# One core, attention and a quantised layer: the transfers of one queue in another order, and the second batch of y transposed by DRAM and VectorE

## What is computed

```python
Q = einsum('btx,dx->btd', layernorm(x), Wq) + bq
K = einsum('bpx,dx->bpd', ctx, Wk) + bk
attn = softmax(einsum('btd,bpd->btp', Q, K) / sqrt(1024))
x1 = x + einsum('btp,bpd->btd', attn, ctx)
w = nibbles of qweight (4 bits); wbin = 1 where w > 0 else -1
weights = scales[g_idx] * (wbin - zeros[g_idx])        # 1024 x 1024
out = x1 + layernorm(x1) @ weights + bias
```

## Time and profile before

| what | value |
|---|---|
| median of 3 runs | 542.48 us (542.15 to 542.54) |
| the profiled execution | 542.7 us, its span 540.9 us, 1.8 us around it |
| PE busy | 534.5 us, 99% of the span |
| DVE, ACT, POOL busy | 371.2, 280.8, 187.2 us (69%, 52%, 35%) |
| granted TensorE clock | 1.00 in the whole span (2.4 GHz) |
| DMA: whole span | 113.38 MB, 210 GB/s |

### The profile page before, as it was taken

The page is one execution under the profiler, slowest core; times in us unless marked ns, Lnnn a source line. Parts: engine busy times, 40 slices in busy tenths (PEclk is TensorE's granted clock), DMA queues, the critical chain, the costliest instruction groups (busy, mean ns, idle before and its releaser), DMA issues.

```text
span 540.9 us, 7404 instructions
## 1 busy us (share of the span) xinstructions
PE 534.5 (99%) x2638; PEld 447.3 (83%) x2638; DVE 371.2 (69%) x604; ACT 280.8 (52%) x496; POOL 187.2 (35%) x151
## 2 busy tenths in 40 slices
PE   8999999999999999999999999999999999999997
PEld 7788788787777877778898899999888888888886
DVE  4988458886888675782446455574968779778742
ACT  5987955314676681343348566686553244325210
POOL 1064000010000000000327777777865744753530
PEclk9999999999999999999999999999999999999999
DMA  8941893459588646936499999898356775774212
GB/s 262 321 163 41 154 158 78 159 147 319 199 237 281 205 173 195 272 83 189 135 213 304 362 321 353 322 417 315 138 150 240 228 225 189 214 233 136 97 79 78
DMA packets 83156, 113.38 MB, mean 210 GB/s; under 512 B 37072, under 2 KB 59672, under 8 KB 80944
## 3 DMA queue, kind: packets, MB, share of 16 engines
q1 hardware_dynamic: 76592, 106.62, 60.7%
q10 hardware_dynamic: 6528, 6.29, 5.8%
HBM read 70.89 MB, written 41.94 MB: 209 GB/s over the span
## 4 chain that ended last, share of the span: by engine, by line
PE 91%; ACT 4%; DMA 2%; DVE 1%; POOL 1%; issue 1%; ACTq 0%; POOLq 0%
PE bank L1395 25%; PE bank L1397 24%; PE bank L1396 24%; PE bank L1433 4%; PE bank L1439 4%; PE bank L1436 4%; PE bank L1485 2%; DMA cin<-in_ctx 2%; POOL cn_lo L613 1%; PE bank L1411 1%; ACT xjunk_early L735 1%; ACT wq_bk L690 1%; ACT xjunk_early L730 1%; PE bank L1544 1%; PE bank L1514 1%
## 5 line engine op out<-in xcount | busy, mean ns | idle before, releaser
L1395 PE MATMUL bank<-xT_hi,m_hi 128*128 128x512 f32 x256 | 101.0, 395 | 0.0
L1397 PE MATMUL bank<-xT_hi,m_lo 128*128 128x512 f32 x256 | 99.7, 390 | 0.0
L1396 PE MATMUL bank<-xT_lo,m_hi 128*128 128x512 f32 x256 | 99.6, 389 | 0.0
L620 POOL TENSOR_TENSOR tT_lo<-t_pair,tT_hi 128x1024 fp32r<-128x1024 f32 x16 | 38.1, 2399 | 75.2 <-ACT tT_hi L662 75.2
L1347 DVE TENSOR_TENSOR xres<-xres,bank 128x512 f32<-128x512 f32 x56 | 38.3, 683 | 36.1 <-PE bank L1397 36.0
L876 ACT ACTIVATE t_pair<-bank,ucol 128x512 f32<-128x512 f32 x32 | 22.0, 687 | 77.7 <-PE bank L1397 73.1
L634 POOL TENSOR_TENSOR l_lo_s<-l_sum_s,l_hi_s 128x512 fp32r<-128x512 f32 x32 | 40.4, 1295 | 54.9 <-DVE l_sum_s L1275 54.9
L1395 PEld LDWEIGHTS bank<-xT_hi,m_hi 128*128 128x128 f32 x256 | 48.0, 188 | 11.8 <-issue 2.1
L1397 PEld LDWEIGHTS bank<-xT_hi,m_lo 128*128 128x128 f32 x256 | 48.0, 188 | 10.2
L1396 PEld LDWEIGHTS bank<-xT_lo,m_hi 128*128 128x128 f32 x256 | 48.1, 188 | 10.0 <-issue 0.2
L1433 PE MATMUL bank<-wk_hi,wq_hi 128*128 128x512 f32 x128 | 50.4, 394 | 0.2
(11 more groups left out here) (158 smaller groups left out, 1246.6 us busy)
## 6 DMA issues: line engine op xcount, KB each, us to landing
xres<-in_x SPq DMA_DIRECT2D x8, 1024.0 KB, 12.4
out<-xres SPq DMA_DIRECT2D x15, 512.0 KB, 5.0
right_scratch<-part_hi SPq DMA_DIRECT2D x28, 256.0 KB, 2.2
xn_scratch<-xin SPq DMA_DIRECT2D x6, 1024.0 KB, 4.7
xq<-xn_scratch ACTq DMA_DIRECT2D x24, 256.0 KB, 5.4
cin<-in_ctx SPq DMA_DIRECT2D x6, 1024.0 KB, 7.2
r_tile<-right_scratch SPq DMA_DIRECT2D x6, 1024.0 KB, 11.1
yn_scratch<-yin SPq DMA_DIRECT2D x6, 1024.0 KB, 4.0
```

The costliest lines, as they stand in the source:

```text
L620: pool.tensor_tensor(tT_lo[b][:, ks, :], t_pair[b // 2][:, b % 2, ks, :], tT_hi[b % 2 if b else 2][:, ks, :].bitcast(F32), ALU.subtract).t ...
L1395: pe.matmul(out_, a_hi, b_hi, start=start, stop=False, skip_group_check=True)
L1396: pe.matmul(out_, a_hi, b_lo, start=False, stop=False, skip_group_check=True)
L1397: return pe.matmul(out_, a_lo, b_hi, start=False, stop=stop, skip_group_check=True)
```

## The change

There are two parts. In the first, SP's transfers stand in another order: the raw x of batch 5 in stage 2 goes behind the store of the normalised batch 4; in stage 3 the first chunk of right factors goes behind the load of ctx of batch 3 instead of ahead of it, the chunks of slices 0 and 1 are one batch later and smaller at the start (three factors at b = 0 in place of five, and two chunks at b = 5), and the bias rows are loaded at b = 6 instead of b = 1. In the second, y of f = 1 is no longer transposed by TensorE but as those of f of 2 and more: stored, read back, and transposed by DVE. For that its statistics move from behind `invert_sum(B - 1)` into batch 6 of attention, POOL's `rsqrt(B + 1)` ahead of `add_bias(0, ..)`, and ACT's `y_apply(1, ..)` ahead of the high parts of s3 and s4 of f = 0. The reloads go out once the last `pv` is done, since `yq` lies where the high part of ctx lay.

```diff
@@ who has made a block of y @@
-            if f < 2:
-                eng.wait_ge(s_ytr, 4 * f + i + 1)
+            if f < 1:
+                eng.wait_ge(s_ytr, i + 1)
             else:
-                eng.wait_ge(s_yb, 4 * (f - 2) + i + 1)
+                eng.wait_ge(s_yb, 4 * (f - 1) + i + 1)
-        RAW = {2: (4, 5), 6: (6,), 12: (7,)}
+        RAW = {2: (4,), 6: (5, 6), 12: (7,)}
@@ SP, attention @@
-            chunks = {0: ((0, 3, 5),), 1: ((0, 5, 7),), 2: ((1, 0, 3),), 3: ((1, 3, 5),), 4: ((1, 5, 7),),
-                      5: ((2, 0, 3),), 6: ((2, 3, 5), (2, 5, 7))}
+            chunks = {0: ((0, 0, 3),), 1: ((0, 3, 5),), 2: ((0, 5, 7),), 3: ((1, 0, 3),), 4: ((1, 3, 5),),
+                      5: ((1, 5, 7), (2, 0, 3)), 6: ((2, 3, 5), (2, 5, 7))}
                 load_x(b)
-                if b == 0:
-                    load_right(0, 0, 3)
                 if b + 3 < B:
                     load_ctx(b + 3)
...
-                if b == 1:
+                if b == 6:
                     sp.dma_start(bias_rows, ...)
@@ SP, quantised layer @@
+            def rows_of_y_by_quadrant(g):
+                sp.wait_ge(s_yn, QT * (g + 1))
+                sp.dma_start(yn_dram[g]..., yin_of(g)).then_inc(s_ynst, 16)
+                sp.wait_ge(s_ynst, 16 * g)
+                if g == 1:
+                    sp.wait_ge(s_pv, 4 * B)
+                else:
+                    sp.wait_ge(s_yb, 4 * (g - 1))
+                for a in range(4):
+                    sp.dma_start(yq[32 * a:32 * a + 32, :, :], ...).then_inc(s_yql[g % 2], 16)
+            rows_of_y_by_quadrant(1)
             for f in range(B):
...
+                if f + 2 < B:
+                    rows_of_y_by_quadrant(f + 2)
@@ POOL @@
                 ctx_lo(b)
+            rsqrt(B + 1)
...
             ctx_lo(B - 1)
-            rsqrt(B + 1)
@@ ACT @@
                 ctx_hi(b)
+            y_apply(1, 1)
+            y_apply(1, 0)
             act.wait_ge(s_cnlo, 4 * B)
             left_hi(0, "s3")
             left_hi(0, "s4")
-            y_apply(1, 1)
-            y_apply(1, 0)
@@ DVE @@
+                if b == B - 2:
+                    dve.wait_ge(s_x1, 4 * (KH + 2))
+                    y_stats(1)
             p_lo(B - 1)
             invert_sum(B - 1)
-            y_stats(1)
...
                 added(f, 3)
+                if f == 0:
+                    y_blocks(1, "a21")
+                    y_blocks(1, "a22")
+                    added(f, 4)
+                    y_blocks(1, "a11")
+                    y_blocks(1, "a12")
                 if f + 1 < B:
                     left_sum(f + 1, "s1")
                     left_sum(f + 1, "s2")
                     left_lo(f + 1, "a11")
-                added(f, 4)
+                if f > 0:
+                    added(f, 4)
@@ PE @@
                     product(b, n)
                     if b == 0 and n == 1:
                         pv(B - 1)
-                    if b == 0 and n == 3:
-                        y_tr(1, ("a21", "a22", "a11", "a12"))
```

More of the change, by code:

```diff
@@ L535, in _ @@
                 load_last_right(n)
-            for f in range(B):
[L539 to L551, removed]
+            def rows_of_y_by_quadrant(g):
+                sp.wait_ge(s_yn, QT * (g + 1))
+                sp.dma_start(yn_dram[g].rearrange("(t p) f -> p t f", p=P), yin_of(g)).then_inc(s_ynst, 16)
+                sp.wait_ge(s_ynst, 16 * g)
[3 more added lines that the diff above has]
+                    sp.wait_ge(s_yb, 4 * (g - 1))
+                rows = yn_dram[g].rearrange("(m j) f -> j m f", j=32)
+                for a in range(4):
+                    sp.dma_start(yq[32 * a:32 * a + 32, :, :], rows[:, :, a * S:(a + 1) * S]
+                                 ).then_inc(s_yql[g % 2], 16)
+            rows_of_y_by_quadrant(1)
+            for f in range(B):
+                if f + 2 < B:
+                    rows_of_y_by_quadrant(f + 2)
                 for t, n in enumerate((5, 6)):
@@ L1289, in y_blocks @@
                 if name == "a21":
-                    dve.wait_ge(s_yql[f % 2], 64 * (f // 2))
+                    dve.wait_ge(s_yql[f % 2], 64 * ((f + 1) // 2))
                     dve.wait_ge(s_lhi, N_PROD * f)
+                    if f == 1:
+                        dve.wait_ge(s_x1, 4 * B)
+                        dve.wait_ge(s_llo_d, 3)
                 dve.transpose(y_bank(f, name)[:, :].rearrange("p (k m j) -> p m k j", k=4, m=4),
@@ L1527, in pv, with y_tr @@
                     ins.then_inc(s_pv, 1)
-            def y_tr(b, names):
+            def y_tr(names):
                 for name in names:
                     t, d = int(name[1]) - 1, int(name[2]) - 1
-                    pe.wait_ge(s_yn, QT * (b + 1))
-                    if b == 0:
-                        pe.wait_ge(s_clo, 4 * B)
-                        if name == "a11":
-                            pe.wait_ge(s_e, QT * (B - 1))
-                        if name == "a12":
-                            pe.wait_ge(s_a21, 1)
-                            pe.wait_ge(s_lsum, 1)
-                    else:
-                        pe.wait_ge(s_x1, 4 * B)
-                        pe.wait_ge(s_llo_d, 3)
+                    pe.wait_ge(s_yn, QT)
+                    pe.wait_ge(s_clo, 4 * B)
+                    if name == "a11":
+                        pe.wait_ge(s_e, QT * (B - 1))
+                    if name == "a12":
+                        pe.wait_ge(s_a21, 1)
+                        pe.wait_ge(s_lsum, 1)
                     for n in range(4):
-                        ins = pe.transpose(y_bank(b, name)[:, n * P:(n + 1) * P],
-                                           yin_of(b)[:, t, (4 * d + n) * P:(4 * d + n + 1) * P], ident)
+                        ins = pe.transpose(y_bank(0, name)[:, n * P:(n + 1) * P],
+                                           yin_of(0)[:, t, (4 * d + n) * P:(4 * d + n + 1) * P], ident)
                     ins.then_inc(s_ytr, 1)
@@ L1568, in scores @@
                         elif b + 1 == B:
-                            y_tr(0, ("a21", "a22") if j == 3 else ("a11", "a12"))
+                            y_tr(("a21", "a22") if j == 3 else ("a11", "a12"))
             for b in range(B):
```

6 lines of the change are left out of this document (2 added, 4 removed).

## The result

The changed kernel took 544.86 us in the median of 13 runs (543.2 to 545.91), the kernel before 542.65 us beside it: a ratio of 1.0039, 95% interval 1.003 to 1.0049. It is slower by 2.2 us. The forecast was 543.4 us, its range ended at 544.5. The profiled run took 545.91 us with a span of 544.1; the forecast for that run was 543.6, so 2.3 us are missing from the sum. One run each of two kernels further down took 1090.15 us; they are left out of every median, range and ratio here, and were not explained.

The account below looks back on a forecast made before the run. TensorE was taken to bound the kernel, waiting only 2.9 us in all. The sum was 542.7 - 1.4 - 0.1 + 2.4 = 543.6 for the profiled execution, which lies 0.2 above the median, so 543.4; range 541.0 to 544.5.

Parts of the forecast that it names:

- The wait for ctx (-1.4): In attention, TensorE's wait at 301.13 for the load of ctx of batch 3 goes away: -1.4 us.
- x (-0.1): TensorE's 0.2 us wait behind a sum needing x of batch 0 may go: -0.1 us, bounds 0 and -0.3.
- The transfers pushed back, "together 0": Right-factor chunks and bias arrive later in SP's queue, but no new wait of TensorE follows: together 0.
- that store itself lands about 3.5 us earlier, having less ahead of it: The last store of x1 lands about 3.5 us earlier, so the last chunk lands near 372 against a need at 376.4.
- the backlog rival: Queued transfers delay the store of y, then reloads, blocks and products; decides from about 1.5 us on: 545 us, chance 0.09.
- The transposes that go (-1.7): Before the first product of f = 1, the 16 transposes leave TensorE: -1.7 us.
- the first product of f = 1 (+0.9): Due at 402.5, it waits 0.8 us for VectorE's low part of a11; the stall costs 0.1 more.
- The port: In f = 1 `nmean` starts 0.1 us behind GpSimd's half of bias and ends with it, a wait of 2.3 us.
- not lost: Rival: `nmean` in f = 1 comes ahead of GpSimd's instruction and is done at once: 541.3 us, chance 0.17.
- a fixed price of 1.0 us: Rival: `nmean` is blocked for a fixed 1.0 us, or its chain begins 1 us earlier: 542.2 us, chance 0.08.
- The wait for n = 4 (+3.0): In f = 1 the product n = 4, due at 414.5, waits 2.9 us for `added(1, 2)`, done at 417.4.
- Nothing later: In later batches VectorE stays about 0.8 us later, `nmean` keeps meeting GpSimd, 1.0 us of cover remains: nothing lost or won.

Follow-up runs that it names:

- the part alone: The kernel before with only the first part of the change, SP's transfers in another order: 540.97 us, ratio 0.9972; measured again, 540.93 us.
- the one best version: The new order, with GpSimd's reciprocal square root ahead of both bias halves in every batch from f=1 on: 540.15 us; again, 540.43 us.
- with the loads ahead of it again: The one best version with the last two loads of r_last put back ahead of the store of y of f = 1: 540.54 us, ratio 0.9955.
- the reciprocal square root first: The changed kernel with POOL's `rsqrt(B + 3)` ahead of both halves of bias in f = 1: 542.34 us, ratio 1.0005.
- The two kernels with additional `bn_stats`: The kernel before with only the first part, plus four or six unused `bn_stats` on VectorE ahead of `added(1, 2)`: 542.56 us with four, 545.82 with six.
- The new order: The changed kernel with the reciprocal square root first, the store of y first, and VectorE's blocks, lows and sums of f=0 and f=1 reordered: 542.13 us.
- six `bn_stats`: The kernel before with only the first part, plus six unused `bn_stats` on VectorE ahead of `added(1, 2)`: 545.82 us, ratio 1.0062.
- the store of y first: The changed kernel with the last two loads of r_last (1 MB) behind the store of y of f = 1: 545.4 us, ratio 1.0052.

## Why the prediction was wrong

- **The wait for ctx (-1.4) and x (-0.1): right.** Ctx was issued at 292.52 and TensorE did not wait; the first product of f = 0 begins at 376.24 instead of 377.82, and the part alone gave -1.4 in the median against the kernel before beside it (540.97 against 542.32), and -1.7 when measured again (540.93 against 542.64). The small wait behind the sum that needs x is back with 0.3 us in the traces of two later kernels with the same transfers, so that it went is not shown to be the change's doing.
- **The transfers pushed back, "together 0": wrong.** The step that failed is "that store itself lands about 3.5 us earlier, having less ahead of it". The store is the last one of x1, line 443. The first two rows are of the kernel before, the next two of the changed one:

```profile
L443 SPq DMA_DIRECT2D x_scratch<-xres x1: 467/467/467, 344.5 to 344.5; - x1
DMA to landing us min/median/max: 9.2/9.2/9.2
```

```profile
L443 SPq DMA_DIRECT2D x_scratch<-xres x1: 467/467/467, 343.0 to 343.0; - x1
DMA to landing us min/median/max: 11.2/11.2/11.2
```

  It landed at 354.2 where it had landed at 353.7. With the 1.5 us that everything moved forward, that is 2 us later, not 3.5 earlier. The last chunk landed at 375.8, 18.0 us behind its issue at 357.8, against a forecast of 372 - 1.5 = 370.5; TensorE, which begins with the right factors at 376.24, still found what it needed. I counted the queue as always full, so that what goes later is only exchanged. The window where attention begins says otherwise, first for the kernel before, then for the changed one:

```profile
284.00:300.00 16.00, 15.75 (x110) 13.84 (x108) 8.21 (x14) 13.47 (x30) 12.65 (x9) 1.00 0.94 324
```

```profile
284.00:300.00 16.00, 16.00 (x114) 14.49 (x114) 8.20 (x14) 13.70 (x30) 13.01 (x9) 1.00 0.88 269
```

  55 GB/s x 16 us = 0.9 MB less were moved. With fewer loads queued early the queue moved less; that this is what stood at the end is argued and not shown, since the first part alone also moved less there (283 GB/s) and had its last load of r_last down at 383.8. The amount varies from run to run too: in two traces of the one best version the last store of x1 had landed at 351.9 and at 353.5. What is shown is the end of it. Between the issue of y's store at 381.3 and its landing at 388.4 the queue moved 1.9 MB, and 1.0 of that is the store; so about 0.8 MB of loads stood ahead of it. With the last 1 MB of r_last behind the store it landed after 4.9 us, with the loads ahead of it again after 7.5. The store was late, the backlog rival's mechanism, with 1.0 us and not 1.5 or more: the reloads had landed at 395.5, where the forecast says 396.3 - 1.5 = 394.8. Everything on VectorE that hangs on them is 0.7 us late: `nmean` at 410.94 for 411.7 - 1.5 = 410.2. That is 0.7 of the missing 2.3 us in the profiled run.
- **The transposes that go (-1.7) and the first product of f = 1 (+0.9): right in kind.** It waits 1.46 us (402.70 against 401.24, counted from when it was due behind the last matmul) instead of 0.9, for the reason just given. The wait for n = 2 did not come (forecast 0.3); one of 0.25 us for n = 6 of f = 0 came in its place, which the blocks on VectorE delay.
- **The port: right, to 0.1 us.** The forecast had `nmean` 0.1 us behind POOL and ending with it; the trace has 0.10 and 2.31 us, and with the reciprocal square root first the time fell by 2.2 to 2.5 us (the 2.1 of the port, and in some runs the half clock with them). The rivals "not lost" and "a fixed price of 1.0 us" are out. In the same trace another `nmean` met a POOL instruction 0.9 us after its start, and stood still for the rest of it only:

```profile
366.33 0.43 DVE L1061 TENSOR_SCALAR nmean<-mv 128x2 f32<-128x2 f32 x1
```

```profile
365.45 2.54 POOL L614 TENSOR_TENSOR cn_lo<-cin,cn_hi 128x512 fp32r<-128x512 f32 x2 [4.05 <-ACT cn_hi L663]
```

- **The wait for n = 4 (+3.0): its length right, its price wrong.** The step that failed is the one from "It waits 2.9 us" to "f = 2 begins at 417.45 + 3 x 2.72 = 425.6": it prices the wait at its length and the three products behind it at full clock. TensorE waited 2.7 us, and then ran 3.4 us at half clock, so that the three products took 9.93 us and not 8.16: 1.8 us more in the profiled run, for which the sum had no term. This is the largest miss, 1.8 of 2.3 us (with the 0.7 of the store, less 0.2 of small terms, the sum is closed). The two kernels with additional `bn_stats` show it without the rest of the change: 1.3 us more of wait, 3.3 us more of time. The 13 runs of the changed kernel fall into two groups by it: five with a granted clock of 0.999 or 1.0, median 543.67, and eight with 0.996 or 0.997, median 545.38. The forecast of 543.4 is the first group; the majority is the second. Why a wait of this length leads to half clock in one run and not in another stays open: only one run has a trace.
- **Nothing later: right** for TensorE in the changed kernel, though not for the reason given: `nmean` does not keep meeting POOL, it takes 0.17 us in each batch behind f = 1. The new order shows how narrow it was: moved by a few us, the next `nmean` met POOL in f = 2.
- **The range.** The forecast of the likeliest case was built with full clock, as were all rivals; the half clock belonged to the forecast itself, since that had a wait of 3 us in it. The range also ended below the 545 that the backlog rival named for itself.

## What to carry to other kernels

A sum over waits is not a sum over times where a wait is long: where a new wait of TensorE comes near the 2.5 us of these traces, price the matmuls behind it at half clock too, and cut such a wait first, because getting under it pays twice (2.2 us for one moved instruction here). Where a short VectorE instruction can fall behind a long one of GpSimd by chance, order them by a dependency that is there anyway, in each repetition and not just in the one where it hurt. When loads are pushed back in a queue, add up the bytes by stretches and see what stands in the queue at the moment when the next urgent store joins it; allow some 1.5 us for what one program's queue varies by from run to run.

## What the runs showed of the hardware that was not expected

- TensorE's granted clock fell to half for 3.4 us at or soon after the end of a wait of 2.5 to 2.6 us: 416.55 resumed, 417.9 at half in the changed kernel, 415.95 and 416.6 with six `bn_stats`. With the store of y first it was at half as soon as TensorE resumed at 415.58 (0.51 from 415.5 to 416.0, 1.00 before that). Behind waits of 1.2 and 1.7 us it stayed at 1.0.
- The four kernels whose traces have a wait of 2.5 or 2.6 us had a granted clock of 0.994 to 0.997 in 8 of 13, 5 of 6, 4 of 6 and 5 of 5 runs. It is not theirs alone: one run in 12 with the reciprocal square root first (546.15 us) and one in 73 of the kernel before (544.9 us) had 0.997 as well. Neither has a trace, so whether they had a long wait is not known.
- A `tensor_scalar` of 128x2 on VectorE took 0.17 us by itself, and 0.43, 0.56, 1.19 or 2.31 us by where it fell in an instruction of GpSimd; it ended with that instruction each time.
